# Adding an expert's two half blocks of rows to the output with one wait per expert instead of one per half

## The reference

```python
logits = jnp.einsum('bsd,de->bse', x, gate_weight)
affinity = jax.nn.softmax(logits, axis=-1).transpose(0, 2, 1)
gating, index = jax.lax.top_k(affinity, k)                   # k = 1250 // 16 * 2 = 156
x_in = jnp.take_along_axis(x[:, None, :, :], index[..., None], axis=2)
h = jax.nn.gelu(jnp.einsum('bekd,edh->bekh', x_in, w1) + b1[None, :, None, :])
x_e = jnp.einsum('bekh,ehd->bekd', h, w2) + b2[None, :, None, :]
weighted = gating[..., None] * x_e
out = out.at[jnp.arange(Bx)[:, None], idx_flat].add(vals_flat)
```

## Time and profile before

| What | Value |
|---|---|
| median of 3 runs | 2626.36 us |
| profiled execution, its own time | 2644.3 us |
| its span, first to last instruction | 2642.6 us |
| mean granted TensorE clock over the span | 0.869 |
| TensorE busy, share of the span | 79% |
| VectorE busy | 60% |
| ScalarE busy | 36% |
| GpSimd busy | 29% |
| loop over experts, from the first gather to the end of the span | 2389.2 to 2642.6 us |

### The profile page before, as it was taken

How to read it: one execution, slowest core, us unless ns; L and a number is a source line. 1 busy time by engine, 2 the same in 40 slices (tenths; PEclk the granted TensorE clock), 3 DMA queues, 4 the chain that set the end, 5 groups by cost and what they waited for, 6 DMA issues and landing times. The chain is left out here.

```text
span 2642.6 us, 36122 instructions
## 1 busy us (share of the span) xinstructions
PE 2096.5 (79%) x10849; PEld 1293.6 (49%) x10850; DVE 1575.0 (60%) x2490; ACT 951.1 (36%) x1768; POOL 773.6 (29%) x707
## 2 busy tenths in 40 slices
PE   4888888888884563999974397999999999436786
PEld 1444444444442563777731244776346874234453
DVE  1289999999995158333346766776566772262111
ACT  4744444444441221555520214663006660011110
POOL 3176676776762000444453000000000000002333
PEclk7989888888887755999988698999999999658899
DMA  4555555555554320677644313000012001254673
GB/s 132 164 136 133 135 132 135 135 133 136 134 134 93 126 108 2 237 261 272 196 131 124 108 41 102 20 19 17 22 42 62 21 1 66 80 189 125 175 210 58
DMA packets 206222, 300.27 MB, mean 114 GB/s; under 512 B 114695, under 2 KB 126674, under 8 KB 202038
## 3 DMA queue, kind: packets, MB, share of 16 engines
q0 software_dynamic: 98272, 142.08, 19.6%
q1 hardware_dynamic: 107862, 157.06, 18.8%
HBM read 243.72 MB, written 54.96 MB: 113 GB/s over the span
## 5 line engine op out<-in xcount | busy, mean ns | idle before, releaser
L565 POOL DMA_INDIRECT p_s<-node_table,p_srci x320 | 467.3, 1460 | 146.1 <-issue 74.2
L1956 PE MATMUL g_psO<-g_h,g_ring 125*125 125x257 f32 x1600 | 373.0, 388 | 20.3 <-DVE g_ring L2088 11.0
L708 PE MATMUL p_psM<-p_msg,p_to 125*32 125x384 f32 x648 | 290.8, 605 | 82.4 <-DVE p_msg L627 43.9
L1956 PEld LDWEIGHTS g_psO<-g_h,g_ring 125*125 125x125 f32 x1600 | 297.1, 190 | 92.9 <-DVE g_stage L2082 26.5
L585 ACT ACTIVATE p_w<-p_psW 125x512 f32<-125x512 f32 x320 | 187.8, 587 | 369.0 <-PE p_psW L700 369.0
L700 PE MATMUL p_psW<-e_w,p_hid 64*125 64x512 f32 x640 | 272.0, 656 | 20.4 <-DMA p_hid<-hidden 7.7
L627 DVE TENSOR_TENSOR p_msg<-p_w,p_s 125x1536 f32<-125x1536 f32 x160 | 273.4, 1750 | 0.0
L712 PE MATMUL p_psM<-p_msg,p_to 125*32 125x256 f32 x648 | 248.6, 473 | 0.0
L711 PE MATMUL p_psM<-p_msg,p_to 125*32 125x256 f32 x648 | 241.0, 460 | 0.0
L710 PE MATMUL p_psM<-p_msg,p_to 125*32 125x256 f32 x648 | 222.8, 478 | 0.0
L590 ACT ACTIVATE p_of<-e_node_ids,e_rise 125x314 bf16<-125x314 f16 x320 | 176.8, 553 | 8.8 <-PE p_psC L717 5.9
(11 more groups left out here) (342 smaller groups left out, 3869.5 us busy)
## 6 DMA issues: line engine op xcount, KB each, us to landing
p_ring<-in_L_ffn_weights SPq DMA_DIRECT2D x32, 1025.0 KB, 7.4
slot_rows<-p_y POOLq DMA_DIRECT2D x70, 256.0 KB, 4.6
p_w1s<-in_L_ffn_w SPq DMA_DIRECT2D x16, 1024.0 KB, 8.6
p_w2s<-in_L_ffn_w SPq DMA_DIRECT2D x16, 1024.0 KB
hidden<-p_h SPq DMA_DIRECT2D x40, 250.0 KB, 3.4
p_hid<-hidden SPq DMA_DIRECT2D x160, 62.5 KB
g_rb<-receiver_rows SPq DMA_DIRECT2D x16, 610.4 KB
p_x<-x SPq DMA_DIRECT2D x3, 2500.0 KB
```

Of the source, the lines that this page charges most:

```text
L565: pool.indirect_dma_start(s[:, b, c, :, :].rearrange("p k u -> p (k u)"), None, node_table, bass.IndirectOffsetOnAxis(ap=srci[:, b, c:c + ...
L708: nc.tensor.matmul(psM[i][0:32, 0:3 * MUL], a, rows_[:, 0:3, :], start=begin, stop=end)
L1956: last = nc.tensor.matmul(psO[0:P, j, 0:HW], ring[:, i % RING, j * P:(j + 1) * P], h[:, s, hd, :], start=s == 0, stop=s == T - 1)
```

## The change

Two waits are altered. Before, POOL waited ahead of every add until the add before it had landed. Now it waits only ahead of half 0 of an expert, for both halves of the expert before. Half 1 follows half 0 as soon as its own `y` is ready. VectorE waited ahead of every write of `y` for the add that had read that half buffer two experts ago. Now it waits ahead of half 0 alone, for both halves of that expert.

```diff
                     for c in range(2):
                         pool.wait_ge(y_ok, 2 * e + c + 1)
-
-                        if e or c:
-                            pool.wait_ge(added, 16 * (2 * e + c))
+                        if e and c == 0:
+                            pool.wait_ge(added, 32 * e)
                         pool.indirect_dma_start(out, bass.IndirectOffsetOnAxis(ap=chosen[:, c, e:e + 1], axis=0),
                                                 y[:, e % 2, c, :], None, compute_op=ALU.add).then_inc(added, 16)
...
                             v.wait_ge(yb_ok, 2 * e + c + 1)
-                            if not new:
-                                v.wait_ge(added, 16 * (2 * (e - 2) + c + 1))
+                            if not new and c == 0:
+                                v.wait_ge(added, 32 * (e - 1))
                             nc.vector.tensor_scalar(y[:, b, c, :], yb[:, b, c, :], gate[:, c, bass.ds(e, 1)], None,
                                                     ALU.mult).then_inc(y_ok, 1)
```

## The result

The changed kernel takes 2602.77 us (median of 4 runs, 2601.14 to 2608.41) against 2624.64 us for the kernel before in the same comparison (4 runs). The ratio is 0.9921, with a 95% interval of 0.9902 to 0.9939. The time lies in the stated range of 2579 to 2608, 12 us above the 2591 forecast.

The account below looks back on a forecast made before the run. POOL's row of adds, each waiting for the one before, was taken to pace the loop at 14.86 us an expert. Savings of 30.8 (experts 2 to 13) and 4.9 (end), 35.7 us off the 2626.4 median, gave 2591 us, range 2579 to 2608.

Parts of the forecast that it names:

- The bound: In the loop, POOL's row of adds paces at 14.86 us an expert, one short add and one long under weights.
- The adds' price in flight: On POOL's queue, a second add in flight costs about 1 us extra, at worst 4.3 us.
- TensorE's pace, 12.5 us: In experts 2 to 13, a gather late by 0.8 us each time gives 12.5 us an expert, saving 30.8 us.
- T: Start of the bias add of an expert's half 1; the second gather was forecast to come at T + 12.7.
- The end: After the last T, POOL issues the last add at T + 1.5 instead of 6.36 us after it, saving 4.9 us.
- VectorE's edit at nothing: VectorE's changed wait before writing y costs nothing, having 10 us of cover; without it, at most 1.8 us an expert.
- Both signs of being wrong: In the profile after: a pair's second add landing over 12 us after first issue, or gathers' landing growing over 2 us.
- the carrying over of the saving to the median: Whole program: the 35.7 us saved in the 2644.3 us profiled execution was taken unscaled from the 2626.36 us median.
- a pace of 13.5 us: Upper side of case 1 in the loop: full extra 1 us and stalls lowering the clock, giving 2603 us.
- The second, TensorE alone: Rival in the loop: gathers come in time, TensorE paces at 11.69 us an expert, 2581 us; chance 0.17.
- The third, adds that serialize: Rival in POOL's queue: an expert's adds serialize, pace 14.0 us, 2611 us; chance 0.15.
- the fifth: Rival: two accumulating transfers hold each other up, a pair takes some 16 us, slower at 2649 us; chance 0.04.

Follow-up runs that it names:

- the second profile of the changed kernel: The changed kernel once more, with one register operation more in a rare branch of the first stage: 2611.71 us, ratio 0.990 to the kernel before.

## Why the prediction was right, and where it was off

**The bound.** It was read rightly: adds in a row, one of each expert's two slowed by the weights. With the weight loads gone the same waits cost 5 us, the end of the loop.

**The adds' price in flight.** I took about 1 us for the second add. Under early gathers the close pairs showed 0.5 us. The longest landings say less: they reach 10.3 us in the second profile of the changed kernel and 10.6 with early gathers, the longest of before were 9.0 to 9.6 in its four profiles, but with VectorE's half alone, where POOL still waits ahead of every add, one took 10.0. The value was about right and perhaps high.

**TensorE's pace, 12.5 us.** Measured 12.79 and, in the second profile, (2565.15 - 2412.31) / 12 = 12.74 us. The reason given, a gather late by 0.8 us each time, is right in the mean and not in its form: TensorE waits 1.0 to 2.1 us every second time. Two errors nearly cancel here, and that the pace came out so close is partly luck. The gather was later than forecast: in the first profile the stalled transposes start at T + 13.0 to T + 13.7, and T + 12.7 had been worked out. But a stall also gives the next gather its time. Two experts together take that start after T and 11.95 us more (2417.77 to 2429.72), so T + 12.7 would have meant (12.7 + 11.95) / 2 = 12.3 us an expert, and not 12.5. With T + 13.0 to T + 13.7 it is 12.5 to 12.8. The saving from expert 1 to 13 was 180.8 - 153.45 = 27.4 us, and 30.8 had been forecast.

**The end.** 6.36 - 1.59 = 4.8 us, where 4.9 had been forecast.

**VectorE's edit at nothing.** Two comparisons on either side of 1 and 0.5 us of waits agree.

**What the profile after was to show.** Most of it came: half 1 of a pair 1.8 to 3.4 us after half 0, transposes 12.79 us apart, a DMA share of 0.80, the last add 1.59 us after the last T. POOL's wait for adds fell further than to half, and the adds' median landing rose to 6.9 us and not to 9. Both signs of being wrong came as well: pairs landed up to 13.4 us after their first issue, and the gathers' median landing grew by 4.9 us, from 3.4 to 8.3. TensorE did not wait as before all the same. It waited for gathers in the loop for 9.6 us in 6 waits, after 31.8 us in 10, since they were issued at T + 5 and no longer up to 15 us after T. The second sign was at odds with the forecast itself, which had the gather take 8.1 us (T + 4.6 to T + 12.7).

**The step that failed is the carrying over of the saving to the median.** The prediction said: "the 17.9 us between them lie over the whole program, and I carry the saving over unscaled". In the loop itself 35.7 us were forecast and 32.4 measured. The medians differ by 21.9 us and by 24.7 in the second comparison, and by 25.9 with POOL's half alone. The time lies in the range all the same because of the room left above for a pace of 13.5 us, which is not what happened. The kernel before is uneven: its runs on one chip reach from 2625 to 2652 us, while those of the changed kernel stay within 7 us and those with early gathers within 3. Its loop has stalls of 6 to 9 us, one, two or three of them. The first is at expert 5 in all four profiles, and the others are at expert 8, 13 or 14, or absent. The profiled executions of before lay 19.7, 10.1 and 8.5 us above the median of their comparison and once 8.1 below. So the one profile was of a long execution against its own timed runs, and a part of what was saved in it is not there to be saved in those.

The cause of the first 19.7 us stays open. Of the 43.3 us between the two first profiles 10.9 lie ahead of the first gather, where nothing was changed. The changed kernel reached that gather at 2378.29 us, and none of the other 12 profiles of any kernel did before 2382.56. The four timed runs of before in the first comparison reach from 2622 to 2627 us, and the medians on the three chips of the later comparisons are 2636 to 2640, where 2644.3 would be nothing unusual. So a difference between chips, or in their condition, can have made much of it. On which chip the first profile and the first timed runs were taken isn't known.

How far that part lies in the loop isn't settled. Only profiled executions show the loop, and its four values for before have a mean of 252 us. With VectorE's half alone, where POOL waits as before, it took 249.0 and 253.5 us. The timed runs suggest 245, as an estimate: 220.4 us for the changed kernel and 24.7 us of difference, if both kernels take equally long ahead of the loop. The stages ahead of the loop differ by up to 8 us between profiled executions of before (2383.59 to 2391.71), so they take part in it.

**The rivals.** The second, TensorE alone, did not come about in the changed kernel and did once the gathers were moved. The third, adds that serialize, wanted 8.9 + 4.3 = 13.2 us for a pair to land, and the fifth 16. The close pairs under the early gathers took 11.0 us in the mean and at most 12.5, and their experts fitted into 11.69 us of pace. The changed kernel's spread pairs took 12.8 to 13.4, but of that 2.9 to 3.4 us went by before half 1 was issued, so its second adds landed 9.5 to 10.0 us after their own issue. Neither rival is what happens.

**The rule against it.** The second half of a pair landed within 11 us of its own issue, after a start with the first in flight, and the two pairs shown took 9.7 and 12.4 us in all, where two long landings one after the other would be 17.4 us. The Trainium skill's rule ("DMA: Bandwidth & Descriptors", rules for kernel authors) that two transfers to disjoint partition halves serialize therefore doesn't tell what this wait cost: what was given back is most of the landing of one of two adds. Whether the data of the two go one after the other no run here shows.

## What to carry to other kernels

A wait between two transfers that don't depend on each other costs up to a whole landing and more where the issuing queue sets the pace, since everything that the same queue would issue next, here the gathers for a later expert, is held back as well. Where another engine sets the pace it costs little: without the weight loads it was 5.2 us, at the end of the loop. After such a wait is gone, look at once for what stands behind the next wait in the queue: moving the gathers one expert earlier gave another 16.6 us. When a forecast has one transfer late for every turn of a loop, ask whether the stall it causes gives the next one its time. When the cost of a chain depends on how transfers happen to fall against each other, one profiled execution may be far from the median, so hold its own time against the spread of the runs before a saving read from it is carried over.

## What the runs showed of the hardware that was not expected

An accumulating indirect DMA of 78 rows of 2 KB lands in 4.0 to 4.7 us when no weights are loaded, and in up to 10.6 us while 2 MB of them are, so other traffic more than doubles it. TensorE's granted clock after a stall is not settled by the length of the stall alone: after stalls of 1.84 and 1.80 us in one execution, 32 products took 4.45 and 6.07 us (granted clock in these stretches 1.00 and 0.73 of full). After the stalls of 6 us and more in the four profiles of the kernel before, they took between 5.55 and 6.95.
